# Giving the second attention its own code: 49 rows, two heads on row halves, values in halves of 256 queries

## What is computed

```python
def heads(x):
    return x.reshape(B, S, HEADS, HEAD_DIM).transpose(0, 2, 1, 3)
q = heads(hidden_states @ Wq + bq)
k = heads(hidden_states @ Wk + bk)
v = heads(hidden_states @ Wv + bv)
scores = jnp.einsum('bhqd,bhkd->bhqk', q, k) / NORM
probs = jax.nn.softmax(scores, axis=-1)
ctx = jnp.einsum('bhqk,bhkd->bhqd', probs, v)
```

## Time and profile before

| | |
|---|---|
| median of 3 runs | 3236.21 us (3226.59 to 3236.48) |
| span of the profiled execution | 3278.2 us |
| TensorE busy in it | 2922.2 us (89%) |
| VectorE busy | 2439.8 us (74%) |
| ScalarE busy | 1849.7 us (56%) |
| GpSimd busy | 1061.6 us (32%) |
| mean granted TensorE clock | 0.906 |
| attention 2, prologue and steps | 1750.0 us to about 2846 us of the span |

### The profile page before, as it was taken

One profiled execution on the slowest core, in us unless ns is written; L12 is line 12 of the kernel. 1 busy time (PEld: TensorE's weight loads), 2 busy tenths in 40 slices (PEclk: granted clock), 3 DMA queues, 4 the chain that ended last, 5 costly groups with the idle time before them and its releaser, 6 DMA issues. The chain is left out here.

```text
span 3278.2 us, 63755 instructions
## 1 busy us (share of the span) xinstructions
PE 2922.2 (89%) x17818; PEld 1147.0 (35%) x17818; DVE 2439.8 (74%) x4430; ACT 1849.7 (56%) x2379; POOL 1061.6 (32%) x1714
## 2 busy tenths in 40 slices
PE   5886999999999999977897999999999999871887
PEld 4664122222222222215652222222222222361666
DVE  4544899999999999933547999999999999451221
ACT  2433376667776677663440677777777777610332
POOL 0012233333333333213232333232333332155665
PEclk9776799999999999998995999999999999965777
DMA  6776554555445554433654622222222222350211
GB/s 126 219 237 184 104 103 98 100 110 107 102 101 100 111 103 100 90 61 121 206 160 98 124 72 70 72 75 75 73 76 75 70 71 63 97 89 12 58 54 35
DMA packets 222364, 327.92 MB, mean 100 GB/s; under 512 B 63820, under 2 KB 150550, under 8 KB 217650
## 3 DMA queue, kind: packets, MB, share of 16 engines
q0 software_dynamic: 79488, 202.00, 27.3%
q1 hardware_dynamic: 142772, 124.60, 14.5%
HBM read 217.71 MB, written 109.19 MB: 100 GB/s over the span
## 5 line engine op out<-in xcount | busy, mean ns | idle before, releaser
L458 ACT ACTIVATE a_probs<-a_psS 128x1024 f32<-128x1024 f32 x1536 | 1488.5, 1021 | 738.5 <-PE a_psS L371 734.0
L503 DVE TENSOR_REDUCE h_halfmax<-a_psR 128x1 f32<-128x512 f32 x1536 | 979.7, 686 | 73.5 <-PE a_psR L353 64.3
L503 DVE TENSOR_REDUCE a_halfmax<-a_psR 128x1 f32<-128x512 f32 x1536 | 984.2, 686 | 63.6 <-PE a_psR L353 54.5
L371 PE MATMUL a_psS<-a_qrows,a_krows 121*128 121x512 f16 (+1 forms) x3072 | 804.2, 383 | 44.8 <-DMA a_qrows<-relh 40.2
L382 PE MATMUL a_psO<-a_probs,a_v 128*32 128x512 f32 x6144 | 824.0, 609 | 1.2 <-ACT a_probs L458 1.2
L353 PE MATMUL a_psR<-h_kmax,h_qmax 64*128 64x512 f16 x1536 | 357.9, 405 | 40.8 <-POOL h_ident L39 40.1
L371 PEld LDWEIGHTS a_psS<-a_qrows,a_krows 121*128 121x128 f16 (+1 forms) x3072 | 241.8, 98 | 417.7 <-issue 161.5
L353 PE MATMUL a_psR<-a_kmax,a_qmax 64*128 64x512 f16 x1536 | 325.6, 393 | 1.8 <-DVE a_halfmax L503 1.4
L353 PEld LDWEIGHTS a_psR<-h_kmax,h_qmax 64*128 64x128 f16 x1536 | 81.9, 93 | 539.1 <-DVE h_halfmax L503 471.6
L353 PEld LDWEIGHTS a_psR<-a_kmax,a_qmax 64*128 64x128 f16 x1536 | 78.9, 93 | 490.4 <-DVE a_halfmax L503 460.1
L185 POOL DMA_DIRECT2D a_qrows<-qk x240 | 124.1, 517 | 264.5 <-PE a_psO L382 262.0
(11 more groups left out here) (185 smaller groups left out, 2755.2 us busy)
## 6 DMA issues: line engine op xcount, KB each, us to landing
a_qrows<-qk POOLq DMA_DIRECT2D x240, 128.0 KB, 4.2
qk<-p_half SPq DMA_DIRECT2D x96, 256.0 KB, 3.3
a_qrows<-rel POOLq DMA_DIRECT2D x96, 256.0 KB, 4.2
a_v<-v POOLq DMA_DIRECT2D x96, 256.0 KB, 3.1
a_krows<-qk POOLq DMA_DIRECT2D x168, 128.0 KB, 4.5
v<-p_v SPq DMA_DIRECT2D x36, 512.0 KB, 5.7
relh<-p_rel SPq DMA_DIRECT2D x48, 256.0 KB
attn<-a_out SPq DMA_DIRECT2D x96, 128.0 KB, 2.3
```

The costliest lines, as they stand in the source:

```text
L371: mm = nc.tensor.matmul(psS[:, (2 * n + j) % 4, :], K[buf][:, h, keys], A[buf][kt % NA][:, h, queries], start=True, stop=True)
L458: nc.scalar.activation(PT[:, blk % 2, 2 * pair:2 * pair + 2, :], psS[:, b0:b0 + 2, :], ACT.Exp, scale=scale).then_inc(exped, 1)
L503: nc.vector.tensor_reduce(mx[:, unit, half:half + 1], psR[:, slot, :], AX.X, ALU.max)\
```

## The change

Attention 2 gets a function of its own, `attention_pairs`; attention 1 is as it was.

- The term low times low is dropped. Three terms of 16 rows and the row of maxima make 49 rows for scores and 48 for maxima, and both use the same two arrays (`A`, `K`), loaded once a step by 12 DMAs (`load_step`).
- The heads lie in two pairs on rows 0 to 63 and 64 to 127. Two score matmuls, one on each row half, go out together, into two banks, with a count each. ScalarE takes the exponential of one head (512 columns) an instruction, four a block. The scores have 3 banks in place of 4.
- A job of maxima is two matmuls, one on each row half, into two banks of a ring of two slots of 1024 columns. VectorE reduces 1024 columns to two values. There are 32 jobs a step, two a block.
- TensorE does per block: two scores, a job, the first 256 queries of the value products of the block before, two scores, the job or jobs left, the other 256 queries.
- The maxima of a step are combined, transposed, copied (now by ScalarE) and sent to the row in two halves of 512 queries, behind blocks 5 and 13. SyncE issues two DMAs for each. The transposes take a score bank in turn.
- The prologue has 22 jobs. The loads of the step after go out at the first block, into the buffers that the step before used, and TensorE waits for them at block 5.

```diff
+def attention_pairs(nc, name, scale, QK, VN, OD, onehot_dram, head, early):
+    TERMS = ((0, 0), (0, 1), (1, 0))
+    R = len(TERMS) * HD
+    PAIRS = GH // 2
+    HALF = PAIRS * 2 * KT // QH
+    PER_BLK = QH * HALF // BLK
+    NEXT = 5
+    AHEAD = NEXT + HALF // PER_BLK
+    EARLY = PER_BLK * (BLK - AHEAD)
+    RING = 2
+    BANKS = 3
...
+        PROLOGUE = HALF + EARLY
...
+            def step(s, u, first):
+                for blk in range(BLK):
+                    if blk == 0 and not first:
+                        pool.wait_ge(scores, s * SCORES + 1)
+                        nc.gpsimd.sem_inc(paced, 1)
+                        head.load_step(pool, s + 1, A[1 - u], K[1 - u], loaded[1 - u])
+                    if blk in (6, 8):
+                        pool.wait_ge(pvdone, s * PVS + blk + 2)
+                        nc.gpsimd.sem_inc(paced, 1)
+                        load_values(s + 1, 1 - u, blk // 2 - 3)
...
+            def row_of_maxima(buf, qh, unit):
+
+                sp.wait_ge(exped, unit + 1)
+                for r in range(2):
+                    row = 64 * r + R
+                    sp.dma_start(A[buf][row:row + 1, :, 512 * qh:512 * qh + 512], MT[PAIRS * r:PAIRS * r + PAIRS, qh, :])\
+                      .then_inc(mrow, 16)
...
+                    for r in range(2):
+                        of = slice(64 * r, 64 * r + R)
+                        mm = nc.tensor.matmul(psR[:, slot, 512 * r:512 * r + 512], A[b][of, pair, q:q + P],
+                                              K[b][of, pair, 512 * kh:512 * kh + 512], start=True, stop=True)
...
+            def two_scores(s, buf, kt, qh, pair, m, first):
+
+                if not (first and m == 0):
+                    pe.wait_ge(exped, s * SCORES + m)
+                keys, queries = slice(P * kt, P * kt + P), slice(512 * qh, 512 * qh + 512)
+                for r in range(2):
+                    of = slice(64 * r, 64 * r + R + 1)
+                    nc.tensor.matmul(psS[:, bank(m + r), :], K[buf][of, pair, keys], A[buf][of, pair, queries],
+                                     start=True, stop=True).then_inc(scores, 1)
...
+                pe.wait_ge(exped, s * SCORES + place(blk, GH - 1, end) + 2)
...
+                cols = slice(256 * part, 256 * part + 256)
+                for h in range(GH):
+                    mm = nc.tensor.matmul(psO[32 * h:32 * h + 32, cols], V[buf][:, kt, h, :],
+                                          PT[:, blk % 2, 2 * (h % 2) + h // 2, cols],
+                                          start=(kt == 0 and part == 0), stop=(kt == KT - 1 and part == 1))
...
+                    for pair in range(PAIRS):
+                        two_scores(s, u, kt, qh, pair, place(blk, 2 * pair, end), start)
+                        for n, j in jobs[u][blk][:1] if pair == 0 else jobs[u][blk][1:]:
+                            job(n, j, base, (n + shift) % RING, u, s * QH)
+                        if pair == 0:
+                            last_values(0)
+                    if blk == NEXT:
+                        m = place(blk, GH)
+                        row(1, m, 2 * s + 2, s * SCORES + (m + 2 - BANKS))
+                    if blk == AHEAD and not end:
+                        m = place(blk, GH)
+                        row(0, m, 2 * s + 3, s * SCORES + (m + 2 - BANKS))
+                    last_values(1)
...
+                    for o in range(GH):
+                        m = place(blk, o, end)
+                        act.wait_ge(scores, s * SCORES + m + 2)
+                        if o == 0:
+                            act.wait_ge(pvdone, s * PVS + blk + 1)
+                        nc.scalar.activation(PT[:, blk % 2, o, :], psS[:, bank(m), :], ACT.Exp, scale=scale)\
+                            .then_inc(exped, 1)
...
+                    nc.vector.tensor_reduce(MX[:, unit:unit + GH - 1:PAIRS, kh], psR[:, slot, :].rearrange("p (r k) -> p r k", r=2),
+                                            AX.X, ALU.max).then_inc(ring_free, 1)
...
-        attention(nc, "a2", False, 1.0 / float(np.sqrt(C)), QK2, None, None, VN2, O2, a["onehot"], head, early)
+        attention_pairs(nc, "a2", 1.0 / float(np.sqrt(C)), QK2, VN2, O2, a["onehot"], head, early)
```

More of the change, by code:

```diff
@@ L1642, in __init__ @@
         self.rel, self.QK, self.RL, self.RLH, self.onehot = rel, QK, RL, RLH, onehot
[L1643 to L1650, removed]
+        if rel:
+            self.AM = [sb(f"qmax0_{h}", [P, 2, L], F16) for h in range(2)]
+            self.KM = sb("kmax0", [P, 2, L], F16)
+            self.MX = sb("halfmax0", [P, GH * KT, 2], F32)
+            self.MC = sb("rowmax", [P, GH * KT], F32)
+            self.MT = sb("rowmaxT", [GH * KT, P], F16)
+            self.ident = sb("ident", [P, P], F32)
+            self.loadedm = sem("loadedm0")
+            self.const_km = sem("const_km0")
+        else:
+            self.A = sb("qrows0", [P, 2, L], F16)
+            self.K = sb("krows0", [P, 2, L], F16)
+            self.loaded = sem("loaded0")
         self.qkst, self.vst, self.xst = sem("qkst"), sem("vst"), sem("xst")
@@ L1660, in wait_projected, with load_step @@
         engine.wait_ge(self.last, self.LAST)
+    def load_step(self, pool, s, A, K, done):
+        for n, (a, k) in enumerate(((0, 0), (0, 1), (1, 0))):
+            for r in range(2):
+                of = slice(64 * r + HD * n, 64 * r + HD * n + HD)
+                pool.dma_start(A[of, :, :], self.QK[s, a, 0].rearrange("(r p d) t -> r d p t", p=2, r=2)[r]).then_inc(done, 16)
+                pool.dma_start(K[of, :, :], self.QK[s, k, 1].rearrange("(r p d) t -> r d p t", p=2, r=2)[r]).then_inc(done, 16)
     def load(self, pool):
@@ L1670, in every @@
             return rows.rearrange("k (o t) -> k o t", o=1).to_broadcast([k, n, t])
-        KM, onehot = self.KM, self.onehot
         pool.wait_ge(self.qkst, 192 + 16)
@@ L1675, in load @@
         if not self.rel:
[L1676 to L1680, removed]
+            self.load_step(pool, 0, self.A, self.K, self.loaded)
             return
+        KM, onehot = self.KM, self.onehot
         for r in range(2):
```

302 lines of the change are left out of this document (added).

## The result

The changed kernel takes **3180.98 us**, the median of four runs (3172.96 to 3185.91), beside 3233.70 for the kernel before, measured with it (four runs, 3226.59 to 3236.48). The ratio is 0.9837, with an interval of 0.9817 to 0.9857: some 53 us faster. The forecast was 115 us. The direction and the mechanism held. More than half of the gain isn't there.

The account below looks back on a forecast made before the run. TensorE's order of work was taken as the bound, with VectorE 8% behind. Savings of 94 us over 24 steps and 21.5 in the prologue made 115, giving 3121 us from the median; range 3085 to 3205.

Parts of the forecast that it names:

- the forecast's own 3085 to 3155: Whole kernel: range around the forecast of 3121 us if no rival case happened, chance 0.63.
- rivals 1 and 2: First: late rows or loads, or slower signals, 3171, chance 0.15. Second: full drain at each shape change, 3198, chance 0.10.
- Pair and block: Attention 2: three nearly equal engine loops of 1.10, 1.13 and 1.15 us; 1.14 a pair, 2.28 a block.
- Step: Attention 2: 36.5 us for 16 blocks plus 3.2 of extras, 39.7 us a step against 43.6.
- The 94 us for 24 steps: Attention 2: saving from steps 3.9 us shorter each, over 24 steps.
- Prologue: Start of attention 2, before the first scores: 22 jobs at 1.13 us, 21.5 us saved; half clock of 13.6 us stays.
- Loads and rows: Attention 2: GpSimd's loads and SyncE's row transfers, costed at nothing because other work covers them, the rows' cover thin.
- The turn of the loop: Step edge in attention 2: within the 1.8 us besides the blocks before the change; no cost listed afterwards.
- the 1.8 us "besides" of the step before: Unchanged kernel, each step outside its 16 blocks: two output jobs, the row job and the loop turn.
- rival 3: TensorE's value products in attention 2: halves do not shrink, 192 us more, 3428, chance 0.07.
- the remark that the clock may fall: TensorE in attention 2: clock falls because the array streams 0.88 of 1.14 us; within a slower case of chance 0.07.
- if a step edge has a gap: Boundary between steps of attention 2: a gap there in the profile would show the forecast wrong; no size given.

Follow-up runs that it names:

- e5: Changed kernel with the middle-step loops of both TensorE and ScalarE in attention 2 written out; 3115.89 us, ratio 0.9629.
- e1: Changed kernel with only TensorE's loop over the 20 middle steps of attention 2 written out; 3174.32 us, ratio 0.9827.
- b3: Kernel before, with attention 2's value products split into two halves in blocks 0 to 11 only; 3230.32 us, one run.
- s1: e1 with 64 idle semaphore increments ahead of ScalarE's loop; 3134.53 us, one run.
- b4: b3 with 128 idle semaphore increments on TensorE ahead of its part of attention 2; 3323.28 us, one run.
- s3: e1 with 192 idle semaphore increments ahead of ScalarE's loop; 3133.48 us, one run.

## Why the prediction came out as it did

Wrong in size: 53 us instead of 115. The measured 3181 us does lie in the stated range of 3085 to 3205, but outside the forecast's own 3085 to 3155, in the part that was there for rivals 1 and 2. Neither of them happened, so that is luck. Each step of the working, against what the runs show:

- **Pair and block.** Forecast 1.14 and 2.28 us; measured 1.11 to 1.15 and 2.26. The price of a shape change (0.32 behind the jobs, 0.31 measured), of a value half (0.56; 0.57) and of the reduction (1.22 long, 1.13 apart) were right. Rivals 2 and 3 fall with them: no full drain, and 256 columns take little more than half of 512. ScalarE's exponentials follow each other at 0.49 where nothing is waited for, as forecast, and at 0.58 to 0.62 where the next scores come in between.
- **Step.** Forecast 39.7; in the changed kernel 39.2 to 39.8 where no loop turns, and 39.5 throughout in e5. The 94 us for 24 steps were right as a price of the work.
- **Prologue.** 21.5 us forecast, 46.4 - 24.05 = 22.4 measured. The half clock behind it lasted 7.5 us, not 13.6; I had said that it stays.
- **Loads and rows.** The thin cover held. TensorE waited for no transfer at blocks 5, 8 or 0, and the pair stayed at 1.11 to 1.15 and not 1.21, so rival 1 is out.
- **The turn of the loop: the step that failed.** The prediction counted it among the 1.8 us "besides" of the step before and then costed it at nothing afterwards. It gave prices and cover to GpSimd's loads and SyncE's rows, but never counted the 8 more value matmuls and 8 more weight loads a block as *code*. It used them only in rival 3, as work for the array. A turn went from 0.21 us to 4.3 to 5.0 on TensorE, with 2.1 to 3.2 on ScalarE beside it (seen in e1), and half clock for 6.8 to 10.2 us behind. Nine turns are 62 us. That 115 - 62 is just the measured 53 is partly chance: without stalls attention 2 gave 121 and not 115 (e5), and the changed kernel began it some 11 us later. None of the rivals was this; the closest was the remark that the clock may fall, whose place was wrong.

That this term is what was missing is shown by e5: with both loops written out the gain is 118 us. From its first job to the end of its last exponential attention 2 takes 1092.3 us before (1750.0 to 2842.3), 1036.2 in the changed kernel (1760.7 to 2796.9) and 971.4 in e5 (1756.5 to 2727.9): 121 us less than before, by a sum that had said 115. The list of what would make the forecast wrong did name it: "if a step edge has a gap".

Some things stay open. In the profiles of the changed kernels attention 2 begins 4 to 18 us later than in those of before (1754 to 1767 us against 1749 to 1750), though the code of attention 1 is the same. Part of it has come by the end of attention 1 (1460 to 1474 us against 1457 to 1462), part in the projection behind it; I haven't found what brings it. Short spells of half clock in attention 1 don't explain it: e5 has 8 and begins 7 us late, b3 has 9 and doesn't. The 0.5 us a step between s1 (40.0) and e5 (39.5), both without a gap, wasn't tested either; in s1 ScalarE still has the register instructions of its loop. And what the clock alone costs of the 62 us, with the stand taken away, wasn't tried.

## What to carry to other kernels

When a change makes a loop's body longer, count its instructions on every engine before and after, and look at the branch of the turn and at the instruction queues in the profile: a wait for "issue" at the head of a body, together with a jump in those queues (0.92 to 2.34 MB here), is code and not data. Then write the loop out, or keep it well under the length where the stall came (here 1790 on TensorE, 314 on ScalarE), on every engine that turns at that point: alone they gave 7 and 9 us, together 65. And where a kernel gets slower or faster by tens of us on an edit that can't matter, think of the place of its loops.

## What the runs showed that I had not expected

- The place of a loop in the code is worth 40 us: 3174 and 3173 us with 0 and 128 idle instructions ahead, 3135 and 3133 with 64 and 192.
- The stand costs most of its length again behind it: 36.3 us standing in all, 26 us more in the time after it, where the granted clock is at its lower level for 6.8 to 10.2 us each time.
- ScalarE's stall doesn't show in its branch record (45 ns), TensorE's does (4645 ns). For ScalarE one has to read the idle time of the first instruction behind it.
- Semaphore increments by themselves are not free. On TensorE 128 in a row took 19.7 us (b4), on ScalarE 64, 128 and 192 took 4.3, 8.9 and 13.2 us (s1 to s3), there in the prologue, where ScalarE had nothing else to do.
- A written-out program shows the size of a block: in e5 a packet of the instruction queue comes every 128 recorded instructions of ScalarE and every 256 of TensorE. With that beat the place of a loop can be counted from a trace.
